# Layer 1 preparation: the second row normalisation moves from VectorE to ScalarE

## The reference, cut to what matters

```python
x = x + s * g                      # s: layer 0 attention, g: silu(layer 0 experts)
xn = _layernorm(x, axis=-1)        # (x - m) / sqrt(v + 1e-5)
s = _L1_attn_ref(xn, ...)
# inside _L1_attn_ref:
#   xn2 = _layernorm(xn, scale, bias)  # (xn-mu)*rsqrt(var+1e-6)*scale + bias
#   q, k, v = xn2 @ wq, xn2 @ wk, xn2 @ wv ; ... + xn2
# the router of the experts reads xn @ Wr
```

## Time and profile before

| what | value |
|---|---|
| median of three runs | 1694.46 us (1690.88 to 1696.72) |
| the profiled execution | 1691.33 us, of which the span of its instructions is 1689.6 us |
| PE busy | 1502.3 us, 89% |
| DVE busy | 1153.9 us, 68% |
| ACT busy | 963.8 us, 57% |
| POOL busy | 806.1 us, 48% |

### The profile page before, as it was taken

One profiled execution on the slowest core, in us unless ns is written; L12 is line 12 of the kernel. 1 busy time (PEld: TensorE's weight loads), 2 busy tenths in 40 slices (PEclk: granted clock), 3 DMA queues, 4 the chain that ended last, 5 costly groups with the idle time before them and its releaser, 6 DMA issues.

```text
span 1689.6 us, 27193 instructions
## 1 busy us (share of the span) xinstructions
PE 1502.3 (89%) x9542; PEld 1127.7 (67%) x9542; DVE 1153.9 (68%) x1805; ACT 963.8 (57%) x1526; POOL 806.1 (48%) x745
## 2 busy tenths in 40 slices
PE   6589999999988289639999999999999999999966
PEld 3277877787777278516777777777777777767621
DVE  6657757756765377486666667777777777767657
ACT  3465576557554255314454567777677776767654
POOL 6424563645452478214324224565555656555420
PEclk9899999999999589859999999999999999999995
DMA  6716455553442579443333355766767667576473
GB/s 227 239 51 169 119 129 143 122 164 71 119 96 42 149 257 351 177 107 111 101 114 98 103 147 158 178 166 168 183 161 183 163 173 190 152 183 159 110 214 137
DMA packets 184232, 257.01 MB, mean 152 GB/s; under 512 B 36000, under 2 KB 116896, under 8 KB 184096
## 3 DMA queue, kind: packets, MB, share of 16 engines
q1 hardware_dynamic: 157216, 219.53, 42.4%
q0 software_dynamic: 26880, 35.73, 11.8%
HBM read 170.10 MB, written 84.56 MB: 151 GB/s over the span
## 4 chain that ended last, share of the span: by engine, by line
PE 38%; SPq 5%; DMA 4%; DVE 4%; ACT 2%; issue 2%; POOL 0%; DVEq 0%; ACTq 0%
PE a_hidden_bank L93 15%; PE a_bank L93 8%; PE a_bank L1567 5%; PE a_max_bank L1536 5%; DMA a_ka<-qk 3%; PE a_score_bank L1557 3%; SPq L1342 2%; SPq L1346 2%; PE a_max_bank L1582 1%; DVE a_w20lo L1873 1%; ACT a_xThi L1715 1%; PE a_bank L1574 1%; DVE a_neg_max L1832 0%; DMA a_qa<-a_ml 0%; ACT a_prob L1693 0%
## 5 line engine op out<-in xcount | busy, mean ns | idle before, releaser
L1693 ACT ACTIVATE a_prob<-a_score_bank 128x1024 f32<-128x1024 f32 x240 | 246.4, 1026 | 250.2 <-PE a_score_bank L1557 208.1
L1832 DVE TENSOR_REDUCE a_neg_max<-a_max_bank 128x2 f32<-128x1024 f32 x249 | 304.2, 1222 | 89.9 <-PE a_max_bank L1536 86.4
L1481 POOL DMA_INDIRECT fs<-a_y,a_token x80 | 126.4, 1579 | 181.3 <-ACT a_y L1741 158.8
L619 POOL DMA_INDIRECT f<-e_ye,c_slot_row x64 | 104.6, 1635 | 128.7 <-ACT e_ye L530 65.8
L1536 PE MATMUL a_max_bank<-a_ka,a_qa 48*128 48x512 f32 x498 | 126.1, 503 | 24.3 <-DVE a_neg_max L1832 13.2
L1567 PE MATMUL a_bank<-a_prob,a_va 128*32 128x512 f32 x1024 | 144.6, 639 | 0.2 <-issue 0.2
L1855 DVE SCALAR_TENSOR_TENSOR a_tg<-a_tg,a_hidden_bank 128x512 f32<-128x512 f32 x112 | 76.8, 686 | 82.7 <-ACT a_tg L1703 78.8
L708 DVE TENSOR_TENSOR e_h<-e_bank,e_sge 128x512 f32<-128x512 f32 x64 | 44.3, 692 | 112.7 <-ACT e_sge L517 112.3
L1557 PE MATMUL a_score_bank<-a_qa,a_ka 50*128 50x512 f32 x480 | 100.5, 414 | 6.7 <-DMA a_qa<-a_ml 4.3
L364 PE MATMUL e_bank<-m_wqkv,x_rows 128*128 128x512 f32 (+1 forms) x256 | 89.3, 492 | 4.7 <-ACT e_qkv L467 3.0
L1536 PEld LDWEIGHTS a_max_bank<-a_ka,a_qa 48*128 48x128 f32 x498 | 47.4, 187 | 68.6 <-DVE a_neg_max L1832 25.5
(11 more groups left out here) (368 smaller groups left out, 4892.6 us busy)
## 6 DMA issues: line engine op xcount, KB each, us to landing
a_raw<-in_W SPq DMA_DIRECT2D x120, 512.0 KB
e_raw<-in_w SPq DMA_DIRECT2D x48, 512.0 KB, 4.0
a_qa<-qk SPq DMA_DIRECT2D x192, 64.0 KB
a_ka<-qk SPq DMA_DIRECT2D x192, 64.0 KB
xs<-c_pad SPq DMA_DIRECT2D x20, 516.0 KB
a_xg<-xs SPq DMA_DIRECT2D x20, 516.0 KB, 4.9
qk<-p_hi SPq DMA_DIRECT2D x32, 256.0 KB, 4.3
qk<-p_lo SPq DMA_DIRECT2D x32, 256.0 KB, 4.9
```

Of the source, the lines that this page charges most:

```text
L619: nc.gpsimd.indirect_dma_start(f_rows, bass.IndirectOffsetOnAxis(k.slot_row[:, e, t:t + 1], 0), ye[:, t, :], None, compute_op=ALU.add).the ...
L1481: nc.gpsimd.indirect_dma_start(f_rows, bass.IndirectOffsetOnAxis(token[x % 4][:, t:t + 1], 0), y[:, t, :], None, compute_op=ALU.add).then_ ...
L1693: nc.scalar.activation(prob[j % 2][:, 2 * p:2 * p + 2, :], score_bank(g, u)[:], ACT.Exp, scale=float(D) ** -0.5).then_inc(p_done, 1)
L1832: nc.vector.tensor_reduce(neg_max[:, g % 2, :, T * p + t], max_bank(g, m)[:], AX.X, ALU.max, negate=True).then_inc(mx_done, 1)
```

## The change

The function `again(n)` leaves DVE's list and stands in ACT's, with the same waits and `activation(Copy, scale=ra)` for `tensor_scalar(mult)`. On DVE it stood behind normalised(0), behind low_xa(0), and at the end of each block. On ACT, again(0) stands behind the three copies of the weights, again(1) behind turned_xa(0) and in front of gate(2), and again(n+2) behind values(n, 1), in front of gate(n+3) and high(n+1, 0).

```diff
+            def again(n):
+                act.wait_ge(xn_done, n + 1)
+                act.wait_ge(ra_done, n + 1)
+                if n >= 2:
+                    act.wait_ge(tr_ps, 2 * (n - 2) + 2)
+                    act.wait_ge(xas_done, n - 1)
+                for t in range(T):
+                    ins = nc.scalar.activation(xa[n % 2][:, t, :], xn[n % 2][:, t, :], ACT.Copy, scale=ra[:, t:t + 1])
+                ins.then_inc(xa_done, 1)
...
                 nc.scalar.activation(parts[0][:], w_[:], ACT.Copy).then_inc(hi_done, 1)
+            again(0)
             turned_xn(0)
             turned_xa(0)
+            again(1)
             for n in range(NB):
...
                 values(n, 0)
                 values(n, 1)
+                if n + 2 < NB:
+                    again(n + 2)
...
-            def again(n):
-                u = n % 2
-                dve.wait_ge(xn_done, n + 1)
-                dve.wait_ge(ra_done, n + 1)
...
-                for t in range(T):
-                    ins = nc.vector.tensor_scalar(xa[u][:, t, :], xn[u][:, t, :], ra[:, t:t + 1], None, ALU.mult)
-                ins.then_inc(xa_done, 1)
...
             normalised(0)
-            again(0)
...
             low_xa(0)
-            again(1)
...
                     low_xa(n + 1)
-                if n + 2 < NB:
-                    again(n + 2)
```

More of the change, by code:

```diff
@@ L1061, in normalised @@
                 ins.then_inc(xn_done, 1)
-            def again(n):
-                u = n % 2
-                dve.wait_ge(xn_done, n + 1)
-                dve.wait_ge(ra_done, n + 1)
-                if n >= 2:
-                    dve.wait_ge(tr_ps, 2 * (n - 2) + 2)
-                    dve.wait_ge(xas_done, n - 1)
-                for t in range(T):
-                    ins = nc.vector.tensor_scalar(xa[u][:, t, :], xn[u][:, t, :], ra[:, t:t + 1], None, ALU.mult)
-                ins.then_inc(xa_done, 1)
             def low(n, i):
```

## The result

The changed kernel takes 1698.17 us (median of 20 runs), the kernel before 1693.63 us (median of 20 runs): ratio 1.0031, 95% interval 1.0020 to 1.0042, so 4.5 us at the medians and 3.4 to 7.1 us by the interval. The profiled execution takes 1695.88 us, its span is 1694.2 us. One of the 20 runs of the changed kernel took 2154.54 us at a granted clock of 0.641 and is left out of the ratio, as are one run of the kernel before (2242.26 us) and one of xa_ahead (1935.38 us) in the experiments.

The account below looks back on a forecast made before the run. The prediction took two paths meeting at residual, DVE's list and POOL's path through ra, again and keep, to bound the loop. Loop +3.6 and start -0.8 made +2.8 us on the 1694.46 us median: 1697.3 us, range 1690.5 to 1703.

Parts of the forecast that it names:

- The price of the work itself: Again's four instructions on ACT: 1.70 us, 0.56 us more than DVE takes.
- The loop, +0.56 us in a clean turn: Blocks 1 to 5: residual gets going 4.47 us behind again's start instead of 3.91, so each turn is 0.56 us longer.
- two paths meet at residual: At DVE's residual, DVE's list meets ra, again, keep with the shared interface, half a microsecond apart; the latter sets 14.12 us.
- A + 4.42: In DVE's list: residual's turn comes 4.42 us after A, the start of again, behind ACT's gate and highs.
- release at A + 4.47: On POOL: keep's products let go of the shared interface 4.47 us after again's start (A), and residual gets going then.
- Three turns at 0.84: Behind blocks 1, 2 and 3, PE's lower clock makes values late: 0.28 us more, so 0.84 us per turn.
- The start, -0.8 us: Start of the stage: POOL's first keep begins later but gets in sooner, -0.8 us, bounds -1.2 and +1.3.
- Nothing behind again(7), nothing on SP and the transfers: Behind again(7) stands no gate, so nothing is lost; no transfer or SP instruction is moved.
- (b): No cost in the loop: +3.6 us shrinks to 0.5 or less, 1693.7 to 1696.2 us; chance 0.17.
- (c): DVE's time was the bound: 9.1 us gained, 1685.4 us; chance 0.05 with anything else that gains.
- (d): PE's clock may stay full, the three 0.84 turns cost 0.56: 1696.5 us; chance 0.56 together with the main case.
- (a): POOL's first keep addition gets in before residual: 0.93 us more in five turns, 1702.0 us; chance 0.22, full or partial.

Follow-up runs that it names:

- xa_ahead: The changed kernel with gate(n+3), then again(n+2), moved in front of values(n, 1) on ACT: 1700.22 against 1693.76 us, ratio 1.0033.
- xa_twice: The kernel before, with again(2) to again(7) each preceded on DVE by four like instructions into an unread tile: 1690.65 us, a single run.
- gate_ahead: The changed kernel with gate(n+3) moved in front of values(n, 1): 1692.36 against 1693.76 us, ratio 0.9991; once more, 1694.46 against 1692.28 us, ratio 1.0001.
- act_only: The kernel before, again left on DVE, plus four unread ACT instructions of the same shape where the change puts again: 1699.82 us, a single run.
- loop_only: The kernel before with only again(2) to again(7) moved to ACT, again(0) and again(1) left on DVE: 1697.44 against 1693.76 us, ratio 1.0023.
- no_gap: gate_ahead with residual's two instructions split into halves (multiply, multiply, add, add): 1703.77 against 1692.28 us, ratio 1.0053.
- before_b: The kernel before, unaltered, run again for a second trace: 1700.01 us, a single run.

## Why the prediction was right or wrong, point by point

**The price of the work itself: right.** 1.70 us were taken for four instructions on ACT, 1.69 to 1.71 were measured.

**The loop, +0.56 us in a clean turn: right in size, wrong in its reason, so luck had a part in it.** The step that failed is "two paths meet at residual", with the path through ra, again and keep's products as the one that sets the 14.12 us. I read it out of two held instructions, 1.75 and 1.32 us, whose ends lay 14.11 us apart. In these turns the end of the fourth product did release residual. But residual doesn't wait for the products as a whole: xa_twice starts them 1.04 us later and residual gets in behind the second of them, and gate_ahead has its xa as late as the changed kernel and loses nothing. What the runs show in its place: DVE is held until the end of the POOL instruction under way, and keep's instructions end every 0.70 us, about 0.13 us ahead of the end the profile gives. With S the start of the first product, the next end is S + 0.70 k - 0.13. The 0.13 us is fitted to these rows. That gives the hold in each kernel:

| trace | S | residual's turn | next end | hold by it | hold measured (duration - 1.22) |
|---|---|---|---|---|---|
| before, turn 1 | 611.82 | 613.97 | k=4, 614.49 | 0.52 | 0.53 |
| before, turn 2 | 625.93 | 628.51 | k=4, 628.60 | 0.09 | 0.10 |
| after | 612.42 | 615.01 | k=4, 615.09 | 0.08 | 0.08 |
| gate_ahead | 613.55 | 615.19 | k=3, 615.52 | 0.33 | 0.34 |
| xa_ahead | 612.87 | 614.99 | k=4, 615.54 | 0.55 | 0.56 |
| xa_twice | 611.52 | 612.61 | k=2, 612.79 | 0.18 | 0.20 |
| act_only (additions, S 616.16) | 616.16 | 616.37 | k=1, 616.73 | 0.36 | 0.39 |

The same rule (the end of the POOL instruction under way) gives the hold within 0.05 us in all 66 turns 0 to 5 of the eleven traces that have the whole of keep and residual in one piece. The steady 14.12 us of before came from this grid: S itself follows from the turn, so a small shift of residual's turn within one POOL instruction changes the hold and not the turn. The change moved residual's turn by +0.99 us (5.59 to 6.58) and cut the hold by 0.45: +0.54 against 0.55 measured. My A + 4.42 for residual's turn was 4.38, so that part of the working stood; the "release at A + 4.47" that I set against it is the end of the fourth product, the right instant under a wrong rule.

**Three turns at 0.84: two right, one mis-sized.** Turns 3 and 5 take 14.97 and 15.00 us, 0.85 and 0.79 over their turns before. That it was three again is in part luck: in the trace of before the late values meet turns 2 to 4, here turns 3 to 5. Turn 4 takes 16.52: the lower clock covered most of the logits and all of the values, so ACT was free 1.96 us behind `ra`, not 0.4; again began 1.88 us later than ra allowed, and 14.67 + 1.88 = 16.55. The term was 0.28 and measured 1.85. That again waits behind PE's values is shown by the rows, but PE is late by itself: its first projection starts at 656.06, 3.33 us behind low_xa in place of 1.28. With high 0 and 1 as far behind it as in the earlier trace rows (1.69 and 3.07 us), residual's turn would come at about 660.4 with again on DVE too, where it came at 661.16. From there 8.00 us and a hold of 0 to 0.6 make a turn of 15.6 to 16.2 us: an estimate, by which 1.5 to 2.1 of the 2.4 us that turn 4 lost are the clock's and not the change's. The sixth turn of xa_ahead, 2.0 us longer though its again didn't wait for PE, agrees. None of the two traces of the kernel before has a fall of the clock that long, so what it would lose is not shown. Nor is whether the change brings such falls; but one of over 6 us within turns 1 to 6 is in all six traces with clean turns of 14.65 us or more (both of the changed kernel, loop_only, act_only, xa_ahead, no_gap), and in none of the seven with shorter turns, where each such fall lasts 3.4 us.

**The start, -0.8 us: right in sign, too small in the first trace** (-1.8, outside my bound of -1.2; -1.0 in the second, -0.1 in gate_ahead_b). I had taken the weights' landing from the one trace as fixed.

**Nothing behind again(7), nothing on SP and the transfers: right** for this kernel (turn 6: 11.99 against 11.98). xa_ahead shows how near the SP queue was.

**Sum.** In the stage 3.2 us against the 2.8 forecast, with two errors that offset each other: 1.6 us too little for turn 4 and 1.0 too little gain at the start (and 0.2 us won in turn 0). By time it is 4.5 us with 3.4 to 7.1 open; the 1.3 us between the stage's 3.2 and the median are not explained by these traces. Of the rivals, (b) and (c) are out, (d) went the other way (the clock took more, not less; at 0.50 for 13.6 us within turns 1 to 6, where it was 10.2 before), and (a) is real but didn't occur here, as residual's turn came 0.08 us ahead of the fourth product's end. The chance of 0.74 for "same" was too high for what I knew: my own main case ended at +2.8 with a scatter of a few us round it, and the bound was at 5.1. What was measured, 3.4 to 7.1 us, lies across that bound.

## What to carry to other kernels

Before an instruction is moved to an engine with idle time, write down what is queued behind its new place: here the moved work, 0.56 us longer than before, cost a clean turn nothing by itself (residual's turn at 5.62 us against 5.59), though it used up the idle time that POOL had, but the gate that it pushed out of its hole cost 0.95, and putting that one instruction in front gave the loss back. A wait on a slow producer should stand behind everything that doesn't need it, yet not ahead of a copy for which the store queue waits. And a steady period is not proof that the path one has in mind sets it: lengthen that path alone and look.

## What the runs showed of the hardware that I had not expected

Where residual meets keep, VectorE and GpSimd hold each other up one instruction at a time. VectorE's 128x1024 instruction with two SBUF inputs (1.22 us alone) was held for the rest of one GpSimd instruction of 0.70 us, 0.08 to 0.56 us in the turns of the table, never for the queue of them. In no_gap GpSimd got in between two VectorE instructions that stood back to back: four of 128x512 took 4.1 us where two of 128x1024 took 3.2. A GpSimd instruction of 0.70 us that met residual lasted 1.72 us in gate_ahead. But the hand-over is not always that even. At the start of the stage of the kernel before, GpSimd's first product waited through three subtractions of 128x512 (L1099) and residual's first instruction, which stood back to back on VectorE and were not held:

```profile
581.14 3.38 POOL L1004 TENSOR_TENSOR p_xas<-p_xa,p_lnw_row 128x256 f32<-128x256 f32 x1 [1.40 <-DVE p_xa L1071]
```

It is the same in before_b, loop_only and xa_twice (3.37 us). Why GpSimd got in at no_gap's halves and not here is open.

In the changed kernel TensorE waited longer ahead of the logits (1.09 us in the turn shown, 0.85 in the earlier trace rows), and its granted clock was 0.78 and then 0.66 in the two stretches of 6 us from 646 us on; whether the one brings the other is open, for all that the long falls keep to the kernels with the longer turns.
